# Masks of the second score pass as a minimum on VectorE, row factors stored with the rows, experts written out

## The chip, the cores and the metric

One core of a Trainium2 chip runs the program. Its engines take their own instruction streams in order and meet through semaphores: PE (TensorE, matrix products into PSUM), DVE (VectorE, elementwise work and reductions), ACT (ScalarE, activations), POOL (GpSimd) and SP (SyncE, which here only issues transfers). The metric is the device time of one execution in microseconds (us), as the median of several runs.

## The reference

32 sequences of 512 tokens with 256 features (D) pass through an embedding, one attention block and one expert block.

```python
h = (tok_table[x] + pos_table[None] + seg_table[seg]) * sqrt(D)
h = h + attention(layernorm(h))
h = h + experts(layernorm(h))
```

Attention: 16 heads of 16 features look at a causal window of 64 to 127 keys (the own block of 64 and the one before). Eight more heads look at 64 latents, which are means over 8 tokens each; a token sees the latents up to its own. Masked scores are minus infinity ahead of the softmax. Both results are gated by a sigmoid of the query, added, and multiplied by `w_out`.

Experts: each of 8 experts in turn takes the 2048 tokens with its highest score among those not yet taken, so expert e+1 is chosen after expert e.

```python
norm = layer_norm(feat, ln_g, ln_b)
scores = norm @ centroids.T
for e in range(8):
    idx = top_k(where(taken, -inf, scores[:, e]), 2048)
    h = layer_norm(feat[idx], ln_g, ln_b)
    out[idx] = feat[idx] + gelu(h @ w1[e] + b1[e]) @ w2[e] + b2[e]
```

`feat` is itself the layer norm of the attention's output added to it, so a row needs its mean and two inverse deviations.

## The kernel before, in words

The program has three stages. **Attention** runs sequence by sequence, written out as 33 passes of `sequence` on each engine (the last pass only finishes sequence 31). **Selection** picks the first expert's tokens. **Experts** runs a loop `Fori(0, E - 1)` on every engine, with the eighth expert written out behind it; while an expert is computed, DVE and PE choose the tokens of the next.

In attention the table `plan` (ten half steps, two for each of five steps s) sets the order on all engines. One step on PE is:

- `top_scores(s)`: scores with queries on the partitions, 64 queries by 128 keys for all heads (s = 0: the latents; s = 1 to 4: the four tiles of 128 tokens, t = s - 1). They serve only to find each query's largest score.
- half step 2s: tasks of `plan`, among them VAL t (`values`: probabilities times values), WO t (output product), MX (transposes the maxima);
- `key_scores(u)` for u = s - 1: the same scores with keys on the partitions, the query's maximum taken off by a row stored in `Qt`;
- half step 2s + 1: more tasks, among them RO t (the remote heads' product).

Masks are added in PSUM by PE itself: ahead of each score pass, `top_scores` and `key_scores` issue two rounds of eight `MATMUL` of a one-hot (`onehot`) with a mask table of 512 columns in bf16 (L983, L988, L1020, L1024). ACT takes the exponential of the second pass (`act_exp`, L684) into `probT` or `latT`, in two halves called pairs. VAL t multiplies them two half steps later (L1060), and waits for the exponentials of tile t and for DVE to have emptied `V_ps`.

DVE, in program order per step: `dve_tops(s)` (maxima of `top_scores`, L1162), `dve_outputs` for VAL (L1210 to L1215), `dve_latents`, `dve_indices`, `dve_embed` (a later sequence's rows), then the tasks that DVE takes from PE: RO (L1183 `r`, L1186 `mix`), WO (L1192 `score`, L1196 `h`, then the statistics L1199 to L1203), PV. PE has three PSUM banks for the tasks (`M_ps`), so the third task behind a WO waits until DVE has read it out.

Row factors: attention stores only the row (`h1`, 256 floats). Its variance goes to `ve_all`; at the end of attention POOL takes the power -0.5 of all 128x128 of them at once (`rs_all`, L614), and DVE multiplies the scores with it (L1469). In the expert stage the rows are gathered by index, and mean and variance are computed a second time: `dve_stats` (L1309 to L1316), `pool_power` (L579), `dve_scales` (L1320, L1321), after which ACT's `act_rows` (L693, L695) may start.

Of the kernel before, what the change touches and what calls it, by code (L numbers as in the profile page):

```python
# [26 lines left out]
P = 128  # L27
D = 256
# [15 lines left out]
TAKEN = -3e38  # L44
GT = 4
# [3 lines left out]
OW = HD + 1  # L49

# [7 lines left out]
def constants(S):  # L58
# [16 lines left out]
    prev_k, diag_k = np.where(r <= q, NEG, 0.0), np.where(r > q, NEG, 0.0)  # L75
    by_query = np.stack([np.concatenate([none, diag_q], 2), np.concatenate([prev_q, diag_q], 2)], 1)
    even_key = np.concatenate([diag_k, prev_k], 2)
    odd_key = np.stack([np.concatenate([none, diag_k], 2), np.concatenate([prev_k, diag_k], 2)], 1)
    step = S // NL
    half, tile, lat = np.arange(2), np.arange(tiles), np.arange(NL)  # L80
    tok = P * tile[None, None, None, :] + W * half[None, :, None, None] + rows[:, None, :, None]
    lat_query = np.where(lat > tok[..., None] // step, NEG, 0.0)
    lat_key = np.where(r > np.arange(S) // step, NEG, 0.0)
    cols = [f(ident), f(parity * HD ** -0.5), f(parity), f(parity * (NL / S)), f(unit), f(before), f(lane), f(i),
            packed(onehot), packed(by_query), packed(even_key), packed(odd_key), packed(lat_query), packed(lat_key)]
# [5 lines left out]
def tower(nc, ins, out, cin, din, widths, SEQS, S, V, F, E):  # L91
# [12 lines left out]
    with ctx:  # L104
# [8 lines left out]
        def sem(name):  # L113
            return ctx.enter_context(nc.semaphore(name))

        h1_rows = nc.dram_tensor("h1_rows", [TOK, D], F32, kind="Internal").ap()
# [11 lines left out]
        (c_ident, c_query, c_parity, c_latent, c_unit, c_before, c_lane, c_part, onehot, by_query, even_key, odd_key,  # L128
         lat_query, lat_key) = (cst[:, int(at[n]):int(at[n + 1])] for n in range(len(widths)))
        onehot = onehot.bitcast(BF16).rearrange("p (r m) -> p r m", r=2)  # L130
        by_query = by_query.bitcast(BF16).rearrange("p (v r k) -> p v r k", v=2, r=2)
        even_key = even_key.bitcast(BF16).rearrange("p (r q) -> p r q", r=2)
        odd_key = odd_key.bitcast(BF16).rearrange("p (v r q) -> p v r q", v=2, r=2)
        lat_query = lat_query.bitcast(BF16).rearrange("p (a r t n) -> p a r t n", a=2, r=2, t=TS)
        lat_key = lat_key.bitcast(BF16).rearrange("p (r q) -> p r q", r=2)
# [17 lines left out]
        h1 = sb("h1", [P, 2, D])  # L153
        st1 = sb("st1", [P, 6])
        mv1 = sb("mv1", [P, 2])
        ve_all = sb("ve_all", [P, NT])
        rs_all = sb("rs_all", [P, NT])
# [33 lines left out]
        st2 = sb("st2", [P, GT, 6])  # L191
        mv2 = sb("mv2", [P, GT, 2])
        ve2 = sb("ve2", [P, 2, GT])
        rs2 = sb("rs2", [P, 2, GT])
        r1 = sb("r1", [P, GT])
        nmr = sb("nmr", [P, 2, GT])
# [58 lines left out]
        hrow = sb("hrow", [P, 2, GT, D])  # L255
# [17 lines left out]
        s_gr = [sem(f"s_gr{q}") for q in range(GT)]  # L273
        s_var2 = sem("s_var2")
        s_rs2 = sem("s_rs2")
        s_scales = sem("s_scales")
# [34 lines left out]
        s_exp = sem("s_exp")  # L311
        s_PV = sem("s_PV")
# [5 lines left out]
        s_rs1 = sem("s_rs1")  # L318
        s_std = sem("s_std")
# [113 lines left out]
        def _(sp):  # L433
# [21 lines left out]
            def store(b, q):  # L455
                m = Misc(b, q % 2)
                for half in plan:
# [35 lines left out]
            with sp.Fori(0, E - 1) as e:  # L493
# [34 lines left out]

        def pool_gather(pool, gi, q, idx, col):
# [7 lines left out]
                bass.IndirectOffsetOnAxis(idx[:, col:col + 1], 0)).then_inc(s_gr[q], 16)  # L537

        def pool_expert(pool, e, last):
            for g in range(GR):  # L540
# [13 lines left out]
                if g + 1 < GR:  # L554
                    pool_power(pool, gi + 1)
                for q in range(GT):
# [3 lines left out]
                    if (g, q) == (GR - 1, 1) and not last:  # L560
                        pool_power(pool, gi + 1)
# [955 lines left out]
```

## Time and profile before

| | |
|---|---|
| median of 3 runs | 3060.79 us (3056.66 to 3068.5) |
| the profiled execution's own time | 3072.49 us |
| its span, first to last instruction | 3070.7 us |
| PE busy | 2708.5 us (88%) |
| DVE busy | 1803.7 us (59%) |
| ACT busy | 1270.0 us (41%) |
| POOL busy | 874.1 us (28%) |

A row of a timeline gives the start in us from the span's start, the duration, the engine, the line of the kernel, the operation, its output and inputs with their shapes, and in brackets how long the engine was idle before it and what ended that. "issue" means that the profile shows nothing the engine waited for. In a row with x2 the duration covers both instructions. Matmul ends are modelled; starts are recorded. PEclk is the share of TensorE's full clock of 2.4 GHz that was granted.

### The profile page before, as it was taken

How to read it: one execution, taken by the hardware profiler on the slowest of the kernel's cores; microseconds unless marked ns; L12 is line 12 of the kernel's file. 1: busy time of each engine (PE TensorE's matmuls, PEld its weight loads, DVE VectorE, ACT ScalarE, POOL GpSimd, SP SyncE). 2: the span in 40 equal slices, each digit the busy share in tenths (PEclk: the TensorE clock that was granted, in tenths of full speed). 3: DMA queues.
4: the chain of work that ended last, by engine and by line, in shares of the span. 5: the costliest groups of instructions: out<-in, count | busy, mean ns of one | idle time of the engine just before them, and what ended most of it. 6: DMA issues, size and time to landing. Idle time of an engine off the chain costs nothing. (4 is left out here: it accounts for less than half of the span.)

```text
span 3070.7 us, 111586 instructions
## 1 busy us (share of the span) xinstructions
PE 2708.5 (88%) x48136; PEld 1876.3 (61%) x48136; DVE 1803.7 (59%) x5986; ACT 1270.0 (41%) x2665; POOL 874.1 (28%) x938
## 2 busy tenths in 40 slices
PE   2899999999999999999999996069999999999998
PEld 1566666666666666667676665036556655655666
DVE  3556556556565565565565643766667576676721
ACT  1444444444444444444444441033434334344343
POOL 2312112113122122121131201124353444534443
PEclk9999999999999999999999997579999999999999
DMA  2000000000000000000000001001120101111020
GB/s 64 21 23 23 21 23 25 20 23 25 22 23 23 21 25 23 23 25 20 23 25 21 23 18 42 0 28 42 47 65 29 60 31 64 54 44 57 31 67 28
DMA packets 56335, 97.59 MB, mean 32 GB/s; under 512 B 10332, under 2 KB 41000, under 8 KB 55752
## 3 DMA queue, kind: packets, MB, share of 16 engines
q0 software_dynamic: 18624, 50.88, 5.8%
q1 hardware_dynamic: 37256, 40.07, 3.9%
q8 instruction: 355, 5.82, 0.8%
q14 instruction: 100, 0.82, 0.1%
HBM read 55.78 MB, written 33.55 MB: 29 GB/s over the span
## 5 line engine op out<-in xcount | busy, mean ns | idle before, releaser
L511 POOL DMA_INDIRECT rows<-in_tok_table,idx_now x132 | 138.3, 1048 | 1355.4 <-DVE hres L1140 1251.3
L900 PE MATMUL banks<-hT,w 128*128 128x512 f32 x1024 | 476.1, 611 | 18.5 <-ACT hT L710 12.1
L1162 DVE TENSOR_REDUCE mx<-banks 128x8 f32<-128x1024 f32 x256 | 301.6, 1220 | 219.0 <-PE banks L1003 219.0
L684 ACT ACTIVATE probT<-banks 128x1024 f32<-128x1024 f32 x256 | 262.5, 1026 | 229.8 <-PE banks L1047 229.8
L721 ACT ACTIVATE hid<-banks,b 128x512 f32<-128x512 f32 x256 | 175.2, 687 | 418.0 <-PE banks L900 417.9
L900 PEld LDWEIGHTS banks<-hT,w 128*128 128x128 f32 x1024 | 188.9, 193 | 224.6 <-issue 209.9
L1060 PE MATMUL V_ps<-Vo,probT 128*64 128x17 f32 x4096 | 270.2, 212 | 3.4 <-issue 3.3
L1060 PE MATMUL V_ps<-Ve,probT 128*64 128x17 f32 x4096 | 270.0, 212 | 3.2 <-issue 2.9
L1060 PEld LDWEIGHTS V_ps<-Ve,probT 128*64 128x64 f32 x4096 | 255.5, 140 | 27.5 <-issue 27.3
L1237 DVE TENSOR_SCALAR_CACHE_REDUCE hits<-act_s,cval 128x128 bf16<-128x128 f32 x960 | 261.2, 342 | 2.3
L1060 PEld LDWEIGHTS V_ps<-Vo,probT 128*64 128x64 f32 x4096 | 255.6, 140 | 3.8 <-issue 3.8
L913 PE MATMUL M_ps<-w,hid 128*128 128x256 f32 x1024 | 231.6, 379 | 0.0
L913 PE MATMUL V_ps<-w,hid 128*128 128x256 f32 x1024 | 231.5, 379 | 0.0
L913 PEld LDWEIGHTS V_ps<-w,hid 128*128 128x128 f32 x1024 | 192.7, 190 | 38.9 <-issue 15.3
L1183 DVE TENSOR_TENSOR r<-M_ps,sg 128x256 f32<-128x256 f32 x128 | 54.4, 425 | 265.0 <-PE M_ps L789 264.0
L913 PEld LDWEIGHTS M_ps<-w,hid 128*128 128x128 f32 x1024 | 190.3, 190 | 23.6
L563 POOL TENSOR_TENSOR orow<-orow,b 128x256 f32<-128x256 f32 x128 | 126.6, 989 | 228.0 <-DVE orow L1355 226.4
L1041 PE MATMUL banks<-Qt,Kt 32*64 32x128 f32 x4096 | 186.6, 283 | 0.6 <-issue 0.6
L650 ACT ACTIVATE low<-M_ps 8x256 f32<-8x256 f32 x128 | 47.7, 372 | 335.0 <-PE M_ps L783 335.0
L1043 PE MATMUL banks<-Qt,Kt 32*64 32x64 f32 x4096 | 175.8, 227 | 3.0 <-issue 3.0
L1041 PEld LDWEIGHTS banks<-Qt,Kt 32*64 32x64 f32 x4096 | 165.1, 131 | 21.8 <-issue 2.4
L567 POOL DMA_INDIRECT out_rows<-orow,idx_cur x128 | 144.6, 1129 | 109.6 <-POOL orow L563 73.4
(227 smaller groups left out, 5676.3 us busy)
## 6 DMA issues: line engine op xcount, KB each, us to landing
h_rows<-h SPq DMA_DIRECT2D x128, 128.0 KB, 2.1
w<-in_w SPq DMA_DIRECT2D x16, 1024.0 KB, 5.4
Qt<-low SPq DMA_DIRECT2D x256, 4.0 KB
rows<-in_tok_table,idx_now POOLq DMA_INDIRECT x132, 3.5
out_rows<-orow,idx_cur POOLq DMA_INDIRECT x128, 2.5
cst<-in_tables SPq DMA_DIRECT2D x1, 1060.5 KB
Gq<-lowl SPq DMA_DIRECT2D x64, 8.0 KB
b<-in_b SPq DMA_DIRECT2D x8, 128.0 KB, 4.8
```

The lines of the kernel that those rows point to most:

```text
L511: nc.gpsimd.indirect_dma_start(rows[:, t, :], None, ins["tok_table"], bass.IndirectOffsetOnAxis(idx_now[:, t:t + 1], 0)).then_inc(s_rows[t ...
L563: nc.gpsimd.tensor_tensor(out=orow[:, q % 2, :], in0=orow[:, q % 2, :], in1=b2[:, :], op=ALU.add).then_inc(s_add, 1)
L567: nc.gpsimd.indirect_dma_start(out, bass.IndirectOffsetOnAxis(idx_cur[:, g * GT + q:g * GT + q + 1], 0), orow[:, q % 2, :], None).then_inc ...
L684: nc.scalar.activation(dst[:, 2 * pair:2 * pair + 2, :], banks[:, 2 * pair:2 * pair + 2, :], ACT.Exp).then_inc(s_exp, 1)
L721: nc.scalar.activation(hid[:, m, :], S_ps[m % 2][:, 0:GT * P], ACT.Gelu_apprx_tanh, bias=b1[:, m:m + 1]).then_inc(s_hid, 1)
L900: mm = nc.tensor.matmul(S_ps[m % 2][:, 0:GT * P], w1[:, c, m * P:(m + 1) * P], hT[g % 2][:, c, :], start=c == 0, stop=c == KC - 1)
L913: mm = nc.tensor.matmul(O_ps[q % 2][:, 0:D], hid[:, m, q * P:(q + 1) * P], w2[:, m, :], start=m == 0, stop=m == FC - 1)
L1041: nc.tensor.matmul(banks[side[0], g, n * P:(n + 1) * P], k[:, W + at_:P + at_], q[:, at_:at_ + P], start=False, stop=n == G - 1)
L1043: nc.tensor.matmul(banks[side[1], g, n * P:n * P + W], k[:, at_:W + at_], q[:, at_:at_ + W], start=False, stop=False)
L1060: nc.tensor.matmul(V_ps[side[a], h * OW:(h + 1) * OW], probT[t % 2][:, g, n * P + a * W:n * P + (a + 1) * W], vals[:, t, h, :], start=True ...
L1162: nc.vector.tensor_reduce(tops.rearrange("p (g h) -> p g h", g=2), banks[:, 2 * pair:2 * pair + 2, :].rearrange("p g (h k) -> p g h k", h= ...
L1237: ins_ = nc.vector.tensor_scalar(hits[:, c, :], act_s[:, :], cval[:, c:c + 1].bitcast(F32), None, ALU.is_ge, ALU.add, accum_out=counts[:, ...
```

## The change

- **Masks of the second pass.** `key_scores` no longer issues mask products (80 `MATMUL` of 512 columns fewer per sequence). Instead DVE takes the minimum of the exponentials with a table of 0 and 3e38 in fp32 (`dve_keep`, two instructions of 128x1024 per pass, ten per sequence), and VAL waits for that (`s_keep`) instead of the exponentials.
- **One round of latent masks.** `top_scores(0)` issues one round of eight mask products instead of two.
- **Factors with the rows.** A stored row has 260 floats: the last four are the factors of the expert stage, written by POOL in `pool_factors` behind each WO (four small operations); POOL also multiplies the scores. `rs_all`, `dve_stats`, `pool_power` and `dve_scales` are gone. SP's store of the row waits for the factors (`s_fac`), ACT waits for the gathered rows alone (`s_gr`).
- **Experts written out.** `Fori` becomes a Python loop on all five engines.

The diff, cut to its core:

```diff
+    keep_key = np.stack([np.where(np.concatenate([upper & prev & first | ~upper & diag, upper & diag | ~upper & prev], 1),
+                                  KEEP, 0.0) for first in (False, True)], 1)
+    keep_lat = np.where(key <= np.arange(S)[None, :] // step, KEEP, 0.0)
...
                         if name == "WO" and m.here(task):
-                            sp.wait_ge(s_mD, m.out(task))
+                            sp.wait_ge(s_fac, TS * (b - lag(task)) + t + 1)
                             sp.dma_start(h1_tiles[:, bass.ds(TS * (b - lag(task)) + t, 1), :],
                                          h1[:, t % 2, :].unsqueeze(1)).then_inc(s_h1out[t % 2], 16)
...
+        def pool_factors(pool, n, t):
+            own = h1[:, t % 2, :]
+            pool.wait_ge(s_var1, n + t + 1)
+            nc.gpsimd.tensor_tensor(out=own[:, D:D + 2], in0=ve1[:, t % 2, :], in1=mhalf[:, :].to_broadcast([P, 2]),
+                                    op=ALU.pow).then_inc(s_rs1, 1)
+            pool.wait_ge(s_rs1, n + t + 1)
+            nc.gpsimd.tensor_scalar(own[:, D + 2:D + 4], own[:, D:D + 2], mv1[:, t % 2, 0:1], -1.0,
+                                    ALU.mult, ALU.mult).then_inc(s_nm1, 1)
+            new = score[:, :, bass.ds(n + t, 1)]
+            nc.gpsimd.tensor_tensor(out=new, in0=new, in1=own[:, D:D + 1].unsqueeze(1).to_broadcast([P, E, 1]),
+                                    op=ALU.mult).then_inc(s_score, 1)
+            pool.wait_ge(s_nm1, n + t + 1)
+            nc.gpsimd.tensor_scalar(own[:, D + 1:D + 2], own[:, D + 1:D + 2], 1.0, None, ALU.add).then_inc(s_fac, 1)
...
-            pool.wait_ge(s_var1, NT)
-            nc.gpsimd.tensor_tensor(out=rs_all[:, :], in0=ve_all[:, :], in1=mhalf[:, :].to_broadcast([P, NT]),
-                                    op=ALU.pow).then_inc(s_rs1, 1)
             pool.wait_ge(s_next, 1)
             for q in range(GT):
                 pool_gather(pool, 0, q, idx_next, q)
-            pool_power(pool, 0)
-            with pool.Fori(0, E - 1) as e:
-                pool_expert(pool, e, False)
-            pool_expert(pool, E - 1, True)
+            for e in range(E):
+                pool_expert(pool, e, e == E - 1)
...
-        def act_rows(act, gi, q, half):
-            if q == 0:
-                act.wait_ge(s_scales, gi + 1)
+        def act_rows(act, gi, pair, q, half):
+            row = hrow[:, half, q, :]
+            act.wait_ge(s_gr[half][q], 16 * pair + 16)
...
             def key_scores(b, par, u, drained):
                 pe.wait_ge(s_max, drained)
                 pe.wait_ge(s_low[u], 32 * b + 32)
                 t = u - 1
-                for r in range(2):
-                    for g in range(G):
-                        for a in range(2):
-                            if u == 0:
-                                nc.tensor.matmul(banks[side[a], g, :], onehot[strip[g], r, :], lat_key[strip[g], r, :],
-                                                 start=r == 0, stop=False)
-                            else:
...
             def values(b, par, t):
                 pe.wait_ge(s_O, TS * b + t + 1)
-                pe.wait_ge(s_exp, 2 * (NU * b + t + 2))
+                pe.wait_ge(s_keep, 2 * (NU * b + t + 2))
...
+        def dve_keep(dve, k, u):
+            for pair in range(2):
+                dve.wait_ge(s_exp, 2 * k + pair + 1)
+                if u == 0:
+                    kept = latT[:, 2 * pair:2 * pair + 2, :]
+                    mask = keep_lat.unsqueeze(1).to_broadcast([P, 2, S])
+                else:
+                    kept = probT[(u - 1) % 2][:, 2 * pair:2 * pair + 2, :].rearrange("p g (n q) -> p (g n) q", q=P)
+                    mask = keep_key[:, min(u - 1, 1), :].unsqueeze(1).to_broadcast([P, 2 * G, P])
+                nc.vector.tensor_tensor(kept, kept, mask, ALU.min).then_inc(s_keep, 1)
...
                     for task in half:
                         dve_misc(dve, m, task, b, q, base)
+                    if n % 2 and (m.old if n == 1 else m.new):
+                        dve_keep(dve, NU * b + n // 2 - 1, (n // 2 - 1) % NU)
...
-            dve.wait_ge(s_rs1, 1)
-            chain(dve, nc.vector.tensor_tensor(score[:, :, :], score[:, :, :],
-                                               rs_all[:, :].unsqueeze(1).to_broadcast([P, E, NT]), ALU.mult), base)
+            dve.wait_ge(s_score, NT)
             chain(dve, nc.vector.tensor_tensor(score[:, :, :], score[:, :, :],
                                                kb[:, :].unsqueeze(2).to_broadcast([P, E, NT]), ALU.add), base)
```

How the instructions move, at the two places that matter most.

DVE, from RO 2 in half step 1 to VAL 3 in half step 2 (`r` and `mix` are RO's two operations, `mx` the maxima of the next tile, `sg` the first operation on VAL's result). Before:

```order
L1183 TENSOR_TENSOR r<-M_ps,sg 128x256 [waits s_misc]
L1186 TENSOR_TENSOR mix<-loc,r 128x256 [waits s_mD]
L1162 TENSOR_REDUCE mx<-banks 128x8 [waits s_S] x2
L1210 TENSOR_SCALAR sg<-gt 128x32 [waits s_PV]
L1211 RECIPROCAL rc<-V_ps 128x24
```

And in the changed kernel:

```order
L1189 TENSOR_TENSOR r<-M_ps,sg 128x256 [waits s_misc]
L1192 TENSOR_TENSOR mix<-loc,r 128x256 [waits s_mD]
L1170 TENSOR_TENSOR probT<-probT,cst 128x1024 [waits s_exp] x2
L1156 TENSOR_REDUCE mx<-banks 128x8 [waits s_S] x2
L1216 TENSOR_SCALAR sg<-gt 128x32 [waits s_PV]
```

The two minima stand behind `mix` and ahead of the maxima. The same five rows follow one another at the other half steps with an RO; in half step 5, which has none, the minima follow `dve_embed`.

POOL, in half steps 8 and 9, where WO 0 falls between two norms (`rs`, `std`, `xn`) of a later sequence. Before:

```order
L511 DMA rows<-in_tok_table,idx_now 128x256
L518 TENSOR_TENSOR rs<-ve,mhalf 128x1
L524 TENSOR_TENSOR std<-ve,rs 128x1
L526 TENSOR_SCALAR xn<-hres,mv,rs 128x256
L518 TENSOR_TENSOR rs<-ve,mhalf 128x1
```

And in the changed kernel:

```order
L510 DMA rows<-in_tok_table,idx_now 128x256
L517 TENSOR_TENSOR rs<-ve,mhalf 128x1
L523 TENSOR_TENSOR std<-ve,rs 128x1
L525 TENSOR_SCALAR xn<-hres,mv,rs 128x256
L532 TENSOR_TENSOR h<-ve,mhalf 128x2
L536 TENSOR_SCALAR h<-h,mv 128x2
L539 TENSOR_TENSOR score<-score,h 128x8
L543 TENSOR_SCALAR h<-h 128x1
L517 TENSOR_TENSOR rs<-ve,mhalf 128x1
```

Four operations are added behind each WO, ahead of the last norm in this case and in a stretch without other POOL work for WO 1 to 3.

## Rows read from the trace of the kernel before

**Rows 1.** Busy time by engine in most of attention; each time with its instruction count

```profile
core 0: us, PE busy (x) PEld busy (x) DVE busy (x) ACT busy (x) POOL busy (x), PEclk, DMA share, GB/s
150.00:1870.00 1720.00, 1616.47 (x41613) 1163.39 (x41619) 1010.11 (x2530) 812.50 (x1780) 350.51 (x464) 0.99 0.08 22
```

**Rows 2.** Timeline of PE: the latents' second pass, mask products and then scores

```profile
1229.86 0.64 PE L1020 MATMUL banks<-cst 32*64 32x512 bf16 x16
1230.32 1.04 PE L1030 MATMUL banks<-Gq,Gk 32*64 32x512 f32 x16
```

**Rows 3.** Timeline of DVE in the setup: 1024 elements, two operands and one

```profile
25.36 1.23 DVE L1382 TENSOR_TENSOR P<-P,segs 128x1024 f32<-128x1024 f32 x1
27.08 0.69 DVE L1385 TENSOR_SCALAR P<-P 128x1024 f32<-128x1024 f32 x1
```

**Rows 4.** Timelines of DVE and PE, step 1: RO 2, maxima, VAL 3, Q 1

```profile
1224.74 0.42 DVE L1186 TENSOR_TENSOR mix<-loc,r 128x256 f32<-128x256 f32 x1
1225.77 2.36 DVE L1162 TENSOR_REDUCE mx<-banks 128x8 f32<-128x1024 f32 x2 [0.60 <-PE banks L1003]
...
1226.10 0.23 PE L1060 MATMUL V_ps<-Ve,probT 128*64 128x17 f32 x1
...
1232.28 1.12 PE L804 MATMUL M_ps<-x1T,wq 128*128 128x512 f32 x2 [0.67 <-DVE h L1196]
```

**Rows 5.** Timelines of DVE and PE, step 2: RO 3, MX 2

```profile
1235.19 0.42 DVE L1186 TENSOR_TENSOR mix<-loc,r 128x256 f32<-128x256 f32 x1
...
1239.69 0.39 PE L783 MATMUL M_ps<-cst,mx 128*8 128x128 f32 x2
```

**Rows 6.** Timelines, steps 3 and 4: top scores 3, VAL 0, RO 0, VAL 1, V 1

```profile
1246.29 0.65 PE L988 MATMUL banks<-cst 32*64 32x512 bf16 x16 [1.46 <-ACT probT L684]
...
1256.42 0.42 DVE L1186 TENSOR_TENSOR mix<-loc,r 128x256 f32<-128x256 f32 x1
...
1257.74 0.23 PE L1060 MATMUL V_ps<-Ve,probT 128*64 128x17 f32 x1
...
1264.28 1.01 PE L816 MATMUL M_ps<-wvg,x1T 128*128 128x296 f32 x3 [0.46 <-DVE h L1196]
```

**Rows 7.** Timelines of DVE and PE, step 0: RO 1, VAL 2

```profile
1268.96 0.42 DVE L1186 TENSOR_TENSOR mix<-loc,r 128x256 f32<-128x256 f32 x1
...
1271.13 0.23 PE L1060 MATMUL V_ps<-Ve,probT 128*64 128x17 f32 x1
```

**Rows 8.** Timelines of DVE and POOL at the end of attention

```profile
1908.53 0.15 DVE L1203 TENSOR_SCALAR ve_all<-mv 128x1 f32<-128x1 f32 x1
...
1909.54 20.75 POOL L614 TENSOR_TENSOR rs_all<-ve_all,mhalf 128x128 f32<-128x128 f32 x1 [134.31 <-DMA h_rows<-h]
...
1931.69 1.22 DVE L1471 TENSOR_TENSOR score<-score,kb 128x1024 f32<-128x1024 f32 x1
```

**Rows 9.** Groups of instructions on POOL: powers of one column, small product

```profile
L518 POOL TENSOR_TENSOR rs<-ve,mhalf 128x1 f32<-128x1 f32 x128 | 73.9, 577 | 2.9
...
L524 POOL TENSOR_TENSOR std<-ve,rs 128x1 f32<-128x1 f32 x128 | 24.1, 188 | 26.4 <-POOL rs L518 20.7 <-PE M_ps L812 4.8 <-PE M_ps L816 0.6
```

**Rows 10.** Timelines of DVE and ACT: the first expert's rows arrive, ACT starts

```profile
2014.20 0.43 DVE L1309 BATCH_NORM_STATS2 st<-hrow 128x6 f32<-128x256 f32 x1 [3.76 <-DMA hrow<-h_rows,idx_next]
...
2021.31 0.60 ACT L693 ACTIVATE y<-hrow,nmr,rs 128x256 f32<-128x256 f32 x1 [116.49 <-DVE nmr L1321]
```

**Rows 11.** Waits of PE in the expert stage: total us, times, longest us

```profile
PE banks L887 <- ACT y L693: 22.9, 20, 11.9
PE M_ps L826 <- DVE hits L1237: 22.8, 14, 2.3
PE M_ps L845 <- DVE ohB L1288: 12.6, 14, 1.4
PE banks L900 <- ACT hT L710: 12.1, 8, 1.6
PE banks L900 <- ACT hid L721: 6.4, 6, 1.4
```

**Rows 12.** Timelines of DVE and PE where the loop turns from expert to expert

```profile
2294.24 0.17 DVE L1328 COPY b<-b_all 128x8 f32 x1 [3.75 <-issue]
...
2299.62 0.18 PE L826 MATMUL M_ps<-counts,onesb 128*128 128x15 bf16 x1 [1.08 <-DVE hits L1237]
```

**Rows 13.** Timelines of POOL in step 4, and of DVE in the expert stage

```profile
1255.30 1.22 POOL L526 TENSOR_SCALAR xn<-hres,mv,rs 128x256 f32<-128x256 f32 x1
...
2061.69 1.10 DVE L1247 TENSOR_TENSOR thr<-thr,delta 128x1 int32<-128x1 int32 x1
```

More of the change, by code:

```diff
@@ L272, in tower @@
         s_cur = sem("s_cur")
[L273 to L276, printed above, removed]
+        s_gr = [[sem(f"s_gr{j}{q}") for q in range(GT)] for j in range(2)]
         s_scaled = sem("s_scaled")
@@ L492, in _ @@
             sp.dma_start(b2[:, :], ins["b2"][0:1, :].to_broadcast([P, D])).then_inc(s_b2, 16)
-            with sp.Fori(0, E - 1) as e:
+            for e in range(E - 1):
                 src1 = w1_v[:, bass.ds(e + 1, 1), :, :].rearrange("p a c f -> p (a c) f")
@@ L604, in sequence @@
                         pool_norm(pool, b + 2, NORM_AT[n], (q + 2) % HB, m)
+                    for task in half:
+                        name, t = task
+                        if name == "WO" and m.here(task):
+                            pool_factors(pool, TS * (b - lag(task)), t)
             sequence(0, 0)
@@ L723, in act_expert @@
                 if g + 1 < GR or not last:
-                    act_group(act, gi + 1, g + 1 if g + 1 < GR else 0)
+                    act_group(act, gi + 1, GR // 2 * e + (g + 1) // 2, g + 1 if g + 1 < GR else 0)
         @block.scalar
@@ L755, in _ @@
             nc.scalar.activation(scr[:, :], c_ident[:, 0:1], ACT.Copy).then_inc(s_hid, 2)
-            act_group(act, 0, 0)
-            with act.Fori(0, E - 1) as e:
-                act_expert(act, e, False)
-            act_expert(act, E - 1, True)
+            act_group(act, 0, 0, 0)
+            for e in range(E):
+                act_expert(act, e, e == E - 1)
         def pe_misc(pe, m, task, b):
@@ L992, in top_scores @@
-                for n in range(2 * TS if s == 0 else G):
-                    j, c = divmod(n, TS if s == 0 else KC)
+                            nc.tensor.matmul(banks[side[a], g, :].rearrange("p (h k) -> p h k", h=G), onehot[strip[g], r, :],
+                                             by_query[strip[g], min(t, 1) if a == 0 else 1, r, :].unsqueeze(1)
+                                             .to_broadcast([32, G, P]), start=r == 0, stop=False)
+                for n in range(G):
+                    j, c = divmod(n, KC)
@@ L1007, in top_scores @@
-                        if g % 2 and n == (2 * TS if s == 0 else G) - 1:
+                            at_ = t * P + a * W
+                            mm = nc.tensor.matmul(banks[side[a], g, n * P:(n + 1) * P],
+                                                  Qt[par][strip[g], j, c, at_:at_ + W],
+                                                  Kt[par][strip[g], j, c, at_:at_ + P], start=False, stop=n == G - 1)
+                        if g % 2 and n == G - 1:
                             mm.then_inc(s_S, 1)
@@ L1109, in _ @@
                 pe_rows(pe, 0, q)
-            with pe.Fori(0, E - 1) as e:
-                pe_expert(pe, e, False)
-            pe_expert(pe, E - 1, True)
+            for e in range(E):
+                pe_expert(pe, e, e == E - 1)
         CH = {"n": 0}
@@ L1285, in dve_choice @@
             elif part == "list":
-                if not (isinstance(n, int) and k < 2):
+                if not (isinstance(n, int) and n == 0 and k < 2):
                     dve.wait_ge(s_used, LC * n + k - 1)
```

193 lines of the change are left out of this document (72 added, 121 removed).

## The prediction

> **What bounds the kernel now.** I read the page first, then busy time by windows, then the timelines of one sequence in the middle, and last the waits. Attention takes 1720 of the span's 3070.7 us in the window that I read, with PE busy 94% of it at a granted clock of 0.99 (2.4 GHz) and DVE 59% [rows 1]. So a microsecond of PE's work is worth a microsecond only where nothing else ends last, and the reader has to look at the few places in a sequence where PE waits for DVE or ACT: ahead of Q 1 for 0.67 us [rows 4], ahead of the top scores 3 for 1.46 [rows 6], ahead of V 1 for 0.46 [rows 6]. There a shorter PE only waits longer. DVE has 41% to spare as an average, but the change puts work on it at fixed places: right between a task's `mix` and the next VAL. How close VAL follows `mix` today is the number that decides.
>
> **PE's products that go.** One pass of masks takes 1230.32 - 1229.86 = 0.46 us from its first product to the first score product [rows 2]. Five such passes, and the one latent round of two (0.23), are 5 x 0.46 + 0.23 = 2.53 us per sequence, 81 us over 32 sequences, if all were on the path.
>
> **DVE's minima that come.** Ten per sequence. The trace of before has no minimum of 128x1024. An fp32 operation of that shape with two operands took 1.23 us, with one operand 0.69 [rows 3]; these are the two bounds. I take 1.23: the mask is a second operand. Two are 2.46, and with a small hand-over to PE (an estimate) VAL can start 2.5 us after `mix` ends. The pair of maxima of as many elements, 2.36 [rows 4], says the same of two in a row. A sequence then goes as follows, each against its own row.
>
> Step 1: `mix` ends at 1224.74 + 0.42 = 1225.16, VAL 3 could start at 1227.66 and started at 1226.10 [rows 4]: **+1.56**. The 0.46 of the second pass isn't won back, since PE waits ahead of Q 1 for DVE, which is as late [rows 4].
>
> Step 2: `mix` ends at 1235.61 [rows 5]. Here the next reader is MX 2, which needs the maxima behind the minima: 1235.61 + 2.5 + 2.36 = 1240.47 against 1239.69 [rows 5], 0.78 late. The mask pass ahead of it gives 0.46: **+0.32**. The top scores 3 that follow wait for ACT's exponentials, which wait for PE's scores, so that wait moves along.
>
> Step 3: half step 5 has no RO, and the minima of tile 0 follow ACT's second half, behind `dve_embed`. They end about 1.3 us after the exponentials, while the mask products of the top scores 3, 1.46 us of waiting included, are still being issued [rows 6]: nothing.
>
> Steps 3 and 4: `mix` ends at 1256.84, VAL 1 could start at 1259.34 and started at 1257.74 [rows 6]: **+1.60**. V 1 waits for DVE's `h` again [rows 6], so the pass's 0.46 goes into that wait.
>
> Step 0: `mix` ends at 1269.38, VAL 2 could start at 1271.88 and started at 1271.13 [rows 7], 0.75 late, less 0.46: **+0.29**. The latents' 0.23 I count as nothing, in the same wait.
>
> The sum is 1.56 + 0.32 + 1.60 + 0.29 = 3.77 us per sequence, **+121 us** over 32. Were the 0.46 won also in the two places where I gave it up, 2.85 and +91; were it won nowhere, 4.69 and +150.
>
> **Selection.** Scores wait now for one power of 128 columns, 20.75 us [rows 8]. Afterwards only the last tile's factors are outstanding. Their power has two columns: one costs 0.577 [rows 9] and a further one 20.75 / 128 = 0.16, so 0.74, and two small operations of 0.19 [rows 9]. With the hand-over of 0.86 between DVE's variance and POOL [rows 8] the addition of `kb` starts at 1908.68 + 0.86 + 0.74 + 0.38 = 1910.66 and not at 1931.69 [rows 8]: **-21 us**, on the path in full, since DVE does nothing else there.
>
> **First expert.** Its rows were there at 2014.20, and ACT began at 2021.31 behind statistics, power and scales [rows 10]. Now ACT waits for the rows alone: **-7 us**.
>
> **Experts.** From the waits of PE [rows 11]: those for `y` are 22.9, of which 11.9 is the first expert's, counted above; 11.0 go, with the statistics. Where the loop turns, DVE stood 3.75 us with nothing that it waited for [rows 12], then seven waits for `hits` of 1.08 each follow [rows 12]: 7.6 go, the other seven stay, as they lie between two rounds of the search. Of `ohB`'s 12.6 I take 9, because DVE gets there about 4 us earlier, and of `hid` all 6.4, which stand at the turn as well. `hT` stays. Sum 34, **-34 us**; bounds: `y` and `hid` alone 17.4, with all of `ohB` and `hT` 50.
>
> **What costs nothing.** The store of a row waits for POOL's factors, about 2 us later; behind it in SP's queue stand loads for a later sequence, and nobody reads the rows before the gathers, some 100 us after the last store [rows 8, 10]. POOL's four operations per WO, 0.74 + 3 x 0.19 = 1.3 us, fit an engine that is busy 350.51 of 1720 us [rows 1]; if they delayed a norm of a later sequence, that has a step to spare. The rows' 16 further bytes ride on DMA that is busy 8% [rows 1]. PE's clock stays where it is, I think: it is 0.99 with a wait of 1.46 in every sequence [rows 1, 6].
>
> **Sum.** 121 - 21 - 7 - 34 = +59 us. The profiled execution took 3072.49 us, 11.7 above the median of 3060.79, so it would take 3131 and the median **3120 us**. The bounds are 91 - 21 - 7 - 50 = +13, 3074, and 150 - 21 - 7 - 17 = +105, 3166.
>
> **Rival: the minima are quick.** At 0.69 each [rows 3] a pair takes 1.08 us less. Then MX 2 and VAL 2 are in time and both passes there win their 0.46; VAL 3 and VAL 1 are 0.48 and 0.52 late. 1.00 - 0.92 = 0.08 per sequence, 3 us, and the rest's 62 remains: **3002 us**, faster. For it speaks that a one-operand form of the same size has that time. Against it: the row of 1.23 has the very form, two operands in fp32, and the pair of maxima is no quicker. It decides below 1.0 us per minimum: each us by which a pair is shorter takes off 4 per sequence, and 62 / 32 = 1.93 is reached when a pair is 0.46 shorter. Chance 0.10; another 0.06 for a smaller gain, 3030 to 3045, if the minima lie between or fewer places wait than I think.
>
> **Rival: nothing measurable.** The delays come to about half, because the later passes hand some slack on to the next step (two of my four terms are below 0.35 already). 121 halved is 60, against the 62 of the rest: **3060 us**. Chance 0.08.
>
> **Rival: minima that POOL holds up.** DVE has an operation of one column that took 1.10 us in the expert stage [rows 13], against 0.15 for one in attention [rows 8]; what held it the rows don't say. If each critical pair of minima were 0.95 us longer, four in a sequence, 32 x 3.8 = 122 us come on top: **3242 us**. Against it: `mix`, which also reads two operands, took its usual 0.42 at 1256.42, while POOL's `xn` ran from 1255.30 to 1256.52, and `xn` its usual 1.22 [rows 6, 13]. That is an overlap of 0.1 us, and the minima run six times as long in a row, so I keep 0.08. The Trainium skill ("GPSIMD Engine Reference", Specifications) says that POOL shares its SBUF interfaces with VectorE, with contention where a VectorE instruction has two SBUF inputs; this speaks against the change, which adds ten such instructions. By that rule, 3242; the little overlap that the trace of before shows bears out nothing of it.
>
> **Rival: the loop's turn isn't the loop.** Were DVE's 3.75 us not from the turn, `hits` and `ohB` stay, and 17 us less are won: 3137. It lies in the range and in the forecast's chance.
>
> **Chances.** The forecast, slower through late VALs, 3074 to 3166, has 0.68. With POOL's hold-up (0.08) slower by over 0.5% has 0.76. I take 0.5%, 15 us, as what a measurement of this kernel can tell from no change. Within it: 0.08. Faster: 0.10 + 0.06 = 0.16. The range from 3030 to 3166 leaves out the quick minima (0.10) and the hold-up (0.08).
>
> **What would show it.** In the changed kernel PE should wait for DVE's minimum (`probT`, L1170) about 1.6 us ahead of VAL 1 and of VAL 3 and 0.3 to 0.75 ahead of VAL 2 and MX 2, with nothing of the kind ahead of VAL 0; the 320 minima should have a mean of about 1.2 us; a sequence should take 3.8 us longer. The addition of `kb` should stand some 2 us behind the last variance, ACT's first `y` at the arrival of its rows, and the 3.75 us on DVE should be gone. I am wrong if the minima take under 1 us, if DVE runs them before the task's `mix`, or if PE's wait for them is as long as I say and a wait elsewhere shrinks by as much: then the period of a sequence shows it.

## The result, and the profile after

The changed kernel takes 3147.26 us (median of 4 runs, 3138.72 to 3156.45) against 3064.64 of the kernel before in the same session (4 runs): a ratio of 1.0267, 95% interval 1.022 to 1.0314. The profiled executions took 3156.45 and 3072.49 us, so 84 us of difference are to be found in the trace. The forecast was +59, slower, and 3120 us; the measured time lies inside the range, in part by luck, as told below.

First the page of the changed kernel, its line of busy times and the granted clock in 40 slices:

```profile
PE 2714.0 (86%) x45320; PEld 1911.6 (61%) x45320; DVE 2097.6 (66%) x5893; ACT 1266.6 (40%) x2659; POOL 1010.5 (32%) x1417
...
PEclk9999999988999998989998999757999999999999
```

PE issues fewer products and is still as busy as before. The window that answers to [rows 1], and a short one in it (columns as there):

```profile
150.00:1870.00 1720.00, 1505.80 (x35571) 1098.39 (x35570) 1252.17 (x2622) 752.13 (x1649) 534.84 (x895) 0.93 0.08 21
1258.80:1265.00 6.20, 6.20 (x77) 4.89 (x82) 4.23 (x11) 0.37 (x1) 0.00 (x0) 0.50 0.01 3
```

In the same 1720 us there are 35571 instructions on PE instead of 41613. Of the 6042 that are missing, 88 in each of some 28 sequences, about 2460, are the mask products that are gone (an estimate); the rest means that fewer sequences fit into the window. The granted clock is 0.93 instead of 0.99. The second row shows how: for 6.2 us in one sequence PE runs at 0.50, which is 1.2 GHz.

PE's waits in that window (waited for, total us, times, longest us):

```profile
PE V_ps L1055 <- DVE probT L1170: 111.1, 77, 1.9
PE banks L1002 <- ACT probT L690: 40.7, 28, 1.5
PE M_ps L788 <- ACT Gk L675: 17.7, 28, 0.6
PE M_ps L809 <- DVE h L1202: 12.3, 18, 0.7
PE M_ps L798 <- DVE mix L1192: 10.7, 28, 0.6
...
PE M_ps L821 <- DVE h L1202: 4.0, 4, 1.3
```

The first line is the wait of the forecast, VAL for the minima. The timeline of DVE and PE in one sequence, for steps 1 (VAL 3), 2 (MX 2), 4 (VAL 1, V 1) and 0 (VAL 2), answers to [rows 4 to 7]:

```profile
1255.29 0.43 DVE L1192 TENSOR_TENSOR mix<-loc,r 128x256 f32<-128x256 f32 x1
1255.63 2.35 DVE L1170 TENSOR_TENSOR probT<-probT,cst 128x1024 f32<-128x1024 f32 x2
...
1258.13 0.20 PE L1055 MATMUL V_ps<-Ve,probT 128*64 128x17 f32 x1 [1.42 <-DVE probT L1170]
...
1274.15 0.27 PE L788 MATMUL M_ps<-cst,mx 128*8 128x128 f32 x1 [0.63 <-ACT Gk L675]
...
1293.82 0.20 PE L1055 MATMUL V_ps<-Ve,probT 128*64 128x17 f32 x1 [1.88 <-DVE probT L1170]
...
1300.27 0.52 PE L821 MATMUL M_ps<-wvg,x1T 128*128 128x296 f32 x1 [0.92 <-DVE h L1202]
...
1307.30 0.20 PE L1055 MATMUL V_ps<-Ve,probT 128*64 128x17 f32 x1 [0.82 <-DVE probT L1170]
```

Ahead of MX 2 the profile names ACT's `Gk`, but before the change MX 2 started at 1239.69 [rows 5], while `Gk` was still running. What MX 2 needs are DVE's maxima, and these end at 1274.00 in the changed kernel, just ahead of 1274.15. The first row is from the changed kernel, the second from the kernel before:

```profile
1271.65 2.35 DVE L1156 TENSOR_REDUCE mx<-banks 128x8 f32<-128x1024 f32 x2
```

```profile
1239.52 0.70 ACT L669 ACTIVATE Gk<-M_ps,cst 128x64 f32<-128x64 f32 x2
```

The end of attention (DVE, POOL) and the start of the first expert (DVE, ACT), answering to [rows 8, 10]:

```profile
2071.57 0.22 DVE L1209 SCALAR_TENSOR_TENSOR ve<-eps,mv 128x2 f32<-128x2 f32 x1
2071.87 0.72 POOL L532 TENSOR_TENSOR h<-ve,mhalf 128x2 f32<-128x2 f32 x1 [4.18 <-DVE ve L1209]
2073.37 1.23 DVE L1452 TENSOR_TENSOR score<-score,kb 128x1024 f32<-128x1024 f32 x1 [1.57 <-POOL score L539]
...
2151.89 0.17 DVE L1300 TENSOR_TENSOR idx_next<-rank,M_ps 128x16 int32<-128x16 f32 x1
...
2156.79 0.60 ACT L699 ACTIVATE y<-hrow 128x256 f32<-128x256 f32 x1 [88.92 <-DMA hrow<-h_rows,idx_next]
```

And the same row of the list of tokens in the kernel before, which the table below needs:

```profile
2010.27 0.17 DVE L1294 TENSOR_TENSOR idx_next<-rank,M_ps 128x16 int32<-128x16 f32 x1
```

From these rows the spans of the stages, against the terms of the forecast:

| stretch | before | after | difference | forecast |
|---|---|---|---|---|
| start to the last variance | 1908.68 | 2071.79 | +163.1 | +121 |
| to the addition of kb | 23.0 | 1.6 | -21.4 | -21 |
| to the end of idx_next | 78.8 | 78.7 | -0.1 | 0 |
| to ACT's first y | 10.9 | 4.7 | -6.1 | -7 |
| to the end of the span | 1049.4 | 997.9 | -51.5 | -34 |
| sum | 3070.7 | 3154.7 | +84.0 | +59 |

So two terms came out as forecast, and two are larger than forecast, with opposite signs.

### The profile page after: what moved, and what is told of

Same layout as the page of the kernel before. It is cut to its first block and busy times, and to the rows that moved or that the text cites. A ratio compares the mean times of both kernels' runs of the same rounds, so it can differ in the third digit from the quotient of the medians.

```text
span 3154.7 us, 104415 instructions
## 1 busy us (share of the span) xinstructions
PE 2714.0 (86%) x45320; PEld 1911.6 (61%) x45320; DVE 2097.6 (66%) x5893; ACT 1266.6 (40%) x2659; POOL 1010.5 (32%) x1417
## 5 line engine op out<-in xcount | busy, mean ns | idle before, releaser
L902 PE MATMUL banks<-hT,w 128*128 128x512 f32 x1024 | 469.7, 607 | 11.2 <-ACT hT L716 10.8
L1055 PE MATMUL V_ps<-Ve,probT 128*64 128x17 f32 x4096 | 296.6, 221 | 128.1 <-DVE probT L1170 127.0
L532 POOL TENSOR_TENSOR h<-ve,mhalf 128x2 f32<-128x2 f32 x128 | 95.0, 742 | 901.4 <-DVE ve L1209 901.4
L1055 PEld LDWEIGHTS V_ps<-Ve,probT 128*64 128x64 f32 x4096 | 286.0, 154 | 154.3 <-issue 154.3
L1170 DVE TENSOR_TENSOR probT<-probT,cst 128x1024 f32<-128x1024 f32 x256 | 304.5, 1220 | 46.0 <-ACT probT L690 45.9
L510 POOL DMA_INDIRECT rows<-in_tok_table,idx_now x132 | 154.6, 1171 | 498.8 <-DVE hres L1134 410.0
L1055 PE MATMUL V_ps<-Vo,probT 128*64 128x17 f32 x4096 | 300.3, 222 | 0.0
L1055 PEld LDWEIGHTS V_ps<-Vo,probT 128*64 128x64 f32 x4096 | 286.8, 155 | 0.0
L1036 PE MATMUL banks<-Qt,Kt 32*64 32x128 f32 x4096 | 204.9, 299 | 0.3 <-issue 0.2
L1038 PE MATMUL banks<-Qt,Kt 32*64 32x64 f32 x4096 | 191.6, 240 | 0.0
```

The lines of the kernel that those rows point to most:

```text
L510: nc.gpsimd.indirect_dma_start(rows[:, t, :], None, ins["tok_table"], bass.IndirectOffsetOnAxis(idx_now[:, t:t + 1], 0)).then_inc(s_rows[t ...
L902: mm = nc.tensor.matmul(S_ps[m % 2][:, 0:GT * P], w1[:, c, m * P:(m + 1) * P], hT[g % 2][:, c, :], start=c == 0, stop=c == KC - 1)
L1036: nc.tensor.matmul(banks[side[0], g, n * P:(n + 1) * P], k[:, W + at_:P + at_], q[:, at_:at_ + P], start=True, stop=True)
L1038: nc.tensor.matmul(banks[side[1], g, n * P:n * P + W], k[:, at_:W + at_], q[:, at_:at_ + W], start=True, stop=True)
L1055: nc.tensor.matmul(V_ps[side[a], h * OW:(h + 1) * OW], probT[t % 2][:, g, n * P + a * W:n * P + (a + 1) * W], vals[:, t, h, :], start=True ...
L1170: nc.vector.tensor_tensor(kept, kept, mask, ALU.min).then_inc(s_keep, 1)
```

## The experiments

Each ratio is against the kernel before, run on the same chip in the same session; the medians of the kernel before were 3066.43 (the first four kernels), 3081.16 (the next four), 3072.45 (the next three) and 3069.45 us (the last).

### Masks back on PE

```diff
-                pe.wait_ge(s_keep, 2 * (NU * b + t + 2))
+                pe.wait_ge(s_exp, 2 * (NU * b + t + 2))
...
-                        dve_keep(dve, NU * b + n // 2 - 1, (n // 2 - 1) % NU)
```

and the 16 mask products per pass in `key_scores` as before.

> The changed kernel with the masks of the second pass back on PE and no minima; all else of the change stays. Theory A (the minima ahead of VAL cost attention, the rest of the change is worth what the other terms said): about 3003 us, that is 62 below the kernel before; a sequence takes 55.9 us again or up to 0.2 less, the granted clock in attention is 0.99, PE waits for no minimum. Rival B (POOL's factors and the later store cost attention too): the sequence stays above 56.5 us and the time above 3030. Rival C (the gains after attention are smaller than the terms): attention as before, but the end at 3025 to 3065.

Measured: 2993.9 us, ratio 0.9756 (0.9737 to 0.9775). The window's clock is 0.99 and no wait for minima is left:

```profile
150.00:1870.00 1720.00, 1612.59 (x41604) 1162.70 (x41605) 1023.28 (x2541) 814.51 (x1784) 529.43 (x952) 0.99 0.08 23
```

POOL is busy 529 us here, PE does about as many products as before, and the last variance comes at 1902.1 us, some 6.5 earlier than before. So factors, the later store and the written-out experts cost attention nothing that can be seen, and all the loss is in the minima. The gain is 72 us by the medians, a little more than the 62 of the terms.

### Minima of 8 columns

```diff
-                    kept = latT[:, 2 * pair:2 * pair + 2, :]
+                    kept = latT[:, 2 * pair:2 * pair + 2, 0:4]
```

and the same for `probT`.

> The changed kernel with each minimum cut from 1024 columns to 8, in its place and with its semaphore; it leaves the masks of the second pass out. Theory A (what costs is how long the minima stand between mix and VAL): the waits for the minima fall from 111 us to under 15, a sequence falls to between 53.4 us (all of the 2.53 us of mask products won) and 55.0 (0.92 won), the time to 2925 to 2975, the granted clock to 0.98 or more. Rival B (DVE is slowed by POOL, or the mere hand-over by one more engine costs): the waits stay above 40 us, the time above 3060. Rival D (the clock falls because PE's mask products are missing): the granted clock stays at 0.93 and the time above 3000.

Measured: 2930.62 us, ratio 0.9534 (0.9503 to 0.9565), for a kernel that leaves the masks of the second pass out; clock 0.99 up to 1700 us, no wait for minima in the list. Without mask products and with the hand-over in place nothing is lost, so neither the hand-over nor the lack of mask products explains the loss or the clock. What costs is the 2.35 us that two full minima stand ahead of VAL. It is also the mark of what free masks would be worth: 63 us below masks on PE.

### The wait filled with products

```diff
+                for _ in range((0, 3, 1, 3)[t]):
+                    nc.tensor.matmul(V_ps[:, 0:D], c_ident, wq[:, 0, :], start=True, stop=True)
                 pe.wait_ge(s_keep, 2 * (NU * b + t + 2))
```

> The changed kernel with products that nothing reads (128x128 by 128x256 in fp32, 0.42 us each) put on PE where it waits for the minima: three ahead of VAL 1 and VAL 3, one ahead of VAL 2. Theory A' (PE's stand ahead of VAL is what lets the granted clock fall to 1.2 GHz for some 6 us of most sequences): the granted clock in attention goes from 0.93 to 0.97 or more, a sequence takes about 2 us less, the time is about 3080. Rival D (the clock falls for want of the mask products, or for another reason): the clock stays at 0.93 and the time at 3147 or up to 20 above.

Measured: 3057.66 us, ratio 0.9959 (0.9943 to 0.9975). Seven useless products per sequence make the changed kernel 90 us faster. The window, and behind it the waits:

```profile
150.00:1870.00 1720.00, 1569.97 (x37938) 1143.89 (x37940) 1317.82 (x2759) 799.55 (x1738) 595.34 (x940) 1.00 0.08 22
```

```profile
PE M_ps L821 <- DVE h L1204: 24.5, 26, 1.3
PE V_ps L1057 <- DVE probT L1172: 21.4, 53, 0.5
PE M_ps L809 <- DVE h L1204: 21.1, 30, 1.0
```

The clock is 1.00. VAL still waits for the minima behind the filling (21.4 us in all), so the filling delays nothing there. This parts the 163 us of attention: here the addition of kb starts at

```profile
1976.35 1.23 DVE L1454 TENSOR_TENSOR score<-score,kb 128x1024 f32<-128x1024 f32 x1 [1.58 <-POOL score L539]
```

which is 1974.8 for the last variance, 66 us later than before. So 66 us, 2.06 per sequence, are the stands themselves, less what the missing mask products give back, and about 97, 3.0 per sequence, are the clock that falls behind the stands.

### First minimum ahead of r

```diff
+                        dve_keep(dve, NU * b + n // 2 - 1, (n // 2 - 1) % NU, (0,))
                     for task in half:
                         dve_misc(dve, m, task, b, q, base)
...
+                        dve_keep(dve, NU * b + n // 2 - 1, (n // 2 - 1) % NU, (1,))
```

> The changed kernel with the first minimum of each pass ahead of the tasks of its half step on DVE (ahead of r and mix) and only the second behind mix; same work. DVE stands idle for 2.2 to 2.7 us ahead of r at three of the four places, so Theory A (place, not amount): VAL 3 and VAL 2 start 1.2 us earlier, VAL 1 does not (there DVE has no idle time); with the clock back a sequence takes about 56 us and the time is 3005 to 3035, with the clock staying at 0.93 about 3065. Rival B (amount: DVE's ten minima cost by their sum, wherever they stand): 3140 to 3155.

Measured: 3059.95 us, ratio 0.9958 (0.9935 to 0.9981), with the clock at 0.95. The same ten minima cost 87 us less, so it is not their amount. The waits show where the rest sits:

```profile
PE M_ps L798 <- DVE mix L1192: 49.4, 29, 2.0
...
PE V_ps L1055 <- DVE probT L1170: 29.6, 59, 0.7
```

Where DVE has no idle time ahead of `r` (half step 7), the earlier minimum pushes `mix`, and PE stands ahead of MT 0, which needs it, and so less ahead of VAL 1.

### Experts written out, alone

```diff
-            with dve.Fori(0, E - 1) as e:
-                dve_expert(dve, e, False, PER2 * e + base)
+            for e in range(E - 1):
+                dve_expert(dve, e, False, base)
```

on the kernel before, and the same on the four other engines.

> The kernel before with nothing changed but the expert loop written out on the five engines. From the addition of kb to the end the changed kernel is 57.7 us shorter than the kernel before, where the terms said 41. Theory A (the terms, the loop's turn on PE's waits only: 7.6 + 9 + 6.4): 23 us less, about 3043. Rival E (the 17 us that were missing in the sum belong to the turn too, since all engines and the clock start again there): 35 to 42 us less, about 3027. Rival F (they belong to the statistics that are gone): 23 us or less here.

Measured: 3068.76 us, ratio 0.9964 (0.9942 to 0.9985), 11 us (5 to 18). PE's waits in the expert stage, to be held against [rows 11]:

```profile
PE banks L887 <- ACT y L693: 23.6, 21, 12.0
PE M_ps L826 <- DVE hits L1237: 18.7, 15, 2.5
PE M_ps L845 <- DVE ohB L1288: 12.8, 14, 1.6
PE banks L900 <- ACT hT L710: 10.8, 8, 1.4
```

`hid` is gone (6.4) and `hits` shorter by 4, but `ohB` stays. DVE's stands of 3.75 us [rows 12], 23.8 in all before, are gone from its waits. In the changed kernel, where the statistics are gone as well, the list reads:

```profile
PE M_ps L831 <- DVE hits L1243: 15.9, 19, 1.9
PE banks L902 <- ACT hT L716: 10.8, 8, 1.4
PE banks L889 <- ACT y L699: 8.1, 4, 5.8
PE banks L902 <- ACT hid L727: 0.4, 1, 0.4
```

So `ohB` does not go with the loop alone; with the statistics gone too, it does. DVE's own waits in the kernel before point to the reason, which no run shows by itself: ahead of the scales DVE stood for POOL's power, with the search for the next expert queued behind it:

```profile
DVE r L1320 <- POOL rs L579: 46.6, 32, 1.8
```

### VAL later on PE

```diff
-            [("MT", 2), ("VAL", 3), ("WO", 2), ("MX", 1)],
+            [("MT", 2), ("WO", 2), ("VAL", 3), ("MX", 1)],
```

in half steps 2 and 8, and VAL 2 behind the ET tasks in half step 0.

> The changed kernel with VAL later in PE's order alone: behind WO in half steps 2 and 8, behind the last two ET in half step 0, so that PE has 1.16 us (0.6 for VAL 2) of other work while DVE takes the minima; DVE's order is as it was. Theory A (VAL starts when the minima end, and Q 1 and V 1 wait for DVE's h, which comes behind VAL's outputs): the waits ahead of VAL fall from 111 us to under 50, those ahead of Q 1 and V 1 rise by about 1.1 us each, the sequence without clock losses stays at 57 to 58 us; 3050 to 3065 where the clock comes back to 0.97 or more, up to 3130 where it does not. Rival G (what PE fills in is simply won): 1.16 x 2 + 0.6 = 2.9 us a sequence, 93 us and the clock: under 3000.

Measured: 3150.67 us, ratio 1.0219 (1.0178 to 1.026). The wait was moved and not removed; PE's waits now begin with

```profile
PE M_ps L821 <- DVE h L1202: 51.3, 28, 2.0
PE M_ps L809 <- DVE h L1202: 47.3, 28, 2.0
```

V 1 and Q 1, as said: 47 and 35 us more than in the changed kernel (4.0 and 12.3), while VAL's own wait for the minima is down to 4.6 us. What fell short is the time: the clock came back only to 0.96, and new waits for POOL's `xn` (19.6 us) and ACT's `mixT` (31.7) appeared.

### VAL and WO exchanged on both engines

```diff
+                    early = [x for x in half if x[0] == "WO" and n in (2, 8)]
+                    for task in early:
+                        dve_misc(dve, m, task, b, q, base)
```

ahead of `dve_outputs`, together with the order of the run before.

> As the kernel with VAL later on PE, and DVE too takes WO's score, h and statistics in half steps 2 and 8 ahead of VAL's outputs instead of behind them. Theory A (both ends of the chain from the minima over VAL, the outputs and h to Q 1 and V 1 have to be opened): waits ahead of Q 1 and V 1 near 0 and ahead of VAL under 50 us, granted clock 0.97 or more, a sequence of 54.5 to 55.5 us, 2945 to 2985. Rival H (DVE, fuller by 12 us a sequence, is the bound now and hands the delay to RT, r and mix): a sequence stays above 56.5, the time above 3010.

Measured: 3158.33 us, ratio 1.0253 (1.0227 to 1.0279), clock 0.93: a miss. The waits of Q 1 and V 1 are gone and VAL waits 4.5 us in all, but PE stands elsewhere:

```profile
PE M_ps L779 <- POOL xn L525: 53.4, 24, 3.2
```

This looked like a lack of room on DVE; a later run, with the ET tasks left in place, shows that it was their move.

### Masks shared between PE and DVE

```diff
+                pe_mask = [not (u == 1 or u != 2 and g < KC) for g in range(G)]
...
+                    if n % 2 and n != 7 and (m.old if n == 1 else m.new):
+                        dve_keep(dve, NU * b + n // 2 - 1, (n // 2 - 1) % NU, (0, 1) if n == 5 else (0,))
```

> The changed kernel with the masks of the second pass shared: DVE takes minima only where it has idle time (both of tile 0, and the first of tile 2, of tile 3 and of the latents, ahead of r), PE adds its mask products for the rest (tile 1, and half of the three others), so PE issues 1.15 us less of them per sequence than the kernel before. Theory A (place decides): no waits for minima, granted clock 0.98 or more; against the kernel with all masks on PE (2994) between 0.46 and 1.15 us a sequence less: 2957 to 2980. Rival B (each minimum costs, wherever it stands): above 2994.

Measured: 2972.31 us, ratio 0.9641 (0.9617 to 0.9666), clock 0.98, no wait for minima: as Theory A said. Five minima per sequence cost nothing where DVE stands idle.

### One minimum more

The same with `u in (1, 3)`, and both minima of half step 9 ahead of `r`.

> The kernel with shared masks, and one minimum more: DVE takes both of tile 2 ahead of r (there it stands idle for 2.7 us), PE adds none of its masks. Theory A (place decides): 0.23 us a sequence less on PE, no wait for the minima, 2960 to 2972. Rival (the second minimum reaches into r and mix, and VAL 2 or the top scores of the latents wait): 2972 to 3000, with a wait for mix or the minima of 0.3 us or more per sequence.

Measured: 2957.78 us, ratio 0.9625 (0.9594 to 0.9655). Its waits show none for minima and 5.5 us in all for `mix`. It is the fastest kernel of the study that leaves nothing out, 3.75% below the kernel before, but its interval and that of the former overlap.

### One latent round, alone

```diff
-                            if s == 0:
+                            if s == 0 and r == 0:
                                 nc.tensor.matmul(banks[side[a], g, :].rearrange("p (j t n) -> p j t n", j=2, t=TS),
-                                                 onehot[strip[g], r, :],
+                                                 ownhot[strip[g], side[a]],
```

> The kernel before with one round of the latents' query masks instead of two, nothing else. The prediction's term: 0.23 us a sequence on PE, swallowed by the wait that follows: 0, ratio 1.000. Rival: won in full, 32 x 0.23 = 7 us, ratio 0.998; the waits of PE for gt ahead of RO then stay as long as before.

Measured: 3070.34 us, ratio 0.999 (0.9972 to 1.0008). The interval holds both 0 and 7 us; this stays undecided.

### VAL and WO exchanged, ET left in place

> As the kernel with VAL later on both engines, but half step 0 as in the changed kernel (VAL 2 between the ET tasks); VAL 1 and VAL 3 alone stand behind WO. In the former PE waited 53 us for POOL's xn, which the minima of half step 9 hold up (std 1.09 instead of 0.18, xn 2.21 instead of 1.22 us beside them), and the clock stayed at 0.93. Theory I (the moved ET tasks ran into the late xn, and that stand let the clock fall): xn waits under 15 us, the wait for the minima about 25 us (VAL 2 alone), clock 0.96 or more, 3000 to 3060. Rival H (DVE is the bound with the minima, wherever VAL stands): 3120 to 3160 with the clock at 0.93 to 0.95.

Measured: 3022.5 us, ratio 0.9841 (0.9805 to 0.9878), clock 0.98; the list has no line for `xn` and 20.1 us for VAL 2 on the minima. Against the changed kernel (1.0267) that is 4.1% less with the same ten minima, and against the run with the ET tasks moved (1.0253) 4.0% less by leaving these in place. Theory I holds in its signs (what made `xn` late is taken up at the end), and Rival H falls: DVE is not the bound. The kernel is that of the run with VAL and WO exchanged on both engines, without its change of half step 0.

### All on DVE, both cures

```diff
+                        dve_keep(dve, NU * b + n // 2 - 1, (n // 2 - 1) % NU, ((0,), (0,), (0, 1), (), (0, 1))[n // 2])
                     for task in half:
```

ahead of the tasks, the remaining minima behind them, with VAL and WO exchanged.

> All masks of the second pass on DVE as in the changed kernel, with both cures: VAL 1 and VAL 3 behind WO on PE and DVE, and the minima ahead of r where DVE stands idle there (both of tile 2, the first of tile 3 and of the latents; those of tile 1 stay behind mix). Theory A (place decides, the amount does not): no wait for the minima ahead of VAL 2, the clock in attention at 0.98 or more, 2940 to 2975, so level with or below the shared masks (2958). Rival (the 2 us stands of PE that the trace gives to issue, or POOL's xn behind the minima, stay): 2980 to 3020.

Measured: 2996.79 us, ratio 0.9767 (0.9751 to 0.9784), a miss: no better than masks on PE, and above the shared masks. The time lies in the rival's range. VAL waits 4.8 us in all for minima and PE 2.5 for `xn`, but the clock is 0.97, and these stay:

```profile
PE M_ps L802 <- ACT mixT L648: 35.6, 63, 0.6
PE banks L992 <- issue: 16.4, 9, 2.2
```

Waits for `mixT` of 31 to 36 us stand in all four kernels in which WO comes ahead of VAL, and in the changed kernel there are none. What PE stands for within the latents' scores stays open.

## Why the prediction was right, and where not

**The minima ahead of VAL: right in mechanism and place.** The pair takes 2.35 us where 2.46 was taken, and VAL 3, VAL 1 and VAL 2 wait 1.42, 1.88 and 0.82 us, where 1.56, 1.60 and 0.75 was said. VAL 0 waits for none, and MX 2 stands 0.63 us where 0.3 to 0.75 was said. The small minima show that the duration ahead of VAL is the cause, the split minima and the shared masks that the place counts and not the number alone.

**"PE's clock stays where it is, I think": wrong, and the largest error.** I had argued from the wait of 1.46 ahead of the top scores 3, beside which the clock stays at 0.99 [rows 1, 6]. With the waits ahead of VAL added the clock falls: after the stand of 1.42 at 1258.13 PE runs at 1.2 GHz from 1258.8 to 1265, and VAL's products take 3.95 us instead of 2.53. Each of the six sequences from 1011 to 1388 us has one to three such stretches; these two follow a VAL 1 at 1166.12, behind a stand of 1.88, and a VAL 3 at 1318.93, behind one of 1.42:

```profile
1167.00:1173.00 6.00, 6.00 (x86) 4.88 (x91) 3.68 (x10) 0.28 (x1) 0.24 (x1) 0.50 0.01 3
1320.50:1326.50 6.00, 6.00 (x57) 3.47 (x55) 4.34 (x13) 0.37 (x1) 0.00 (x0) 0.50 0.01 3
```

Filling the waits restored the clock and 90 us. This is about 97 of the 163 us, a term that the sum did not have.

**The sum of the stands, 3.77 per sequence: too large.** With the clock held up they cost 2.06, and the term that was off is VAL 2's +0.29. The stretch from V 1 to the next Q 0, in which VAL 2 lies, is 1.26 us shorter in the filled kernel than before (means of 29 sequences: 13.11 and 14.37), while the rest of the sequence is 3.11 longer, where the other three terms make 3.48 (together 1.85 for the sequences between 150 and 1870 us). One such stretch before, V 1 and Q 0:

```profile
1264.28 0.52 PE L816 MATMUL M_ps<-wvg,x1T 128*128 128x296 f32 x1 [0.46 <-DVE h L1196]
...
1278.24 0.59 PE L804 MATMUL M_ps<-x1T,wq 128*128 128x512 f32 x1
```

And in the filled kernel:

```profile
1304.14 0.52 PE L821 MATMUL M_ps<-wvg,x1T 128*128 128x296 f32 x1 [0.93 <-DVE h L1204]
...
1317.06 0.59 PE L809 MATMUL M_ps<-x1T,wq 128*128 128x512 f32 x1
```

The pass (0.46) and the latents' round (0.23), which go there, are 0.69 of it; why the rest goes is not shown. Q 1 and V 1 won nothing, as said: Q 1 follows the start of VAL 3 after 5.82 to 5.96 us in 22 of 26 sequences before and after 5.82 or 5.83 in 29 of 30 of the filled kernel. (The 6.18 of [rows 4] is one of the exceptions.) In step 2 the size was right and the place wrong: the only pass between VAL 3 and MX 2 is that of [rows 2], given up in step 1, but the pass behind MX 2 is won (MX 2 to K 0: 1239.69 to 1241.86 before, 1277.93 to 1279.68 filled).

**Selection and first expert: right** (-21.4 for -21, -6.1 for -7).

**Experts, -34: too small, -51.5, and one reason of it was wrong.** PE's waits less the first expert's fell by 35.5 us, so the sum of the waits was right, though not its parts: `ohB` lost all of its 12.6 and `y` 8.7 of 11.0. But "7.6 go" for `hits` and 9 for `ohB` "because DVE gets there about 4 us earlier" at the turn is not how: writing the loop out alone is worth 11 us, leaves `ohB` at 12.8 and `hits` at 18.7. `ohB` is gone only where the statistics are, behind whose wait for POOL the search stood. The 16 us above the waits lie in PE's busy time, which fell from 973.5 to 958.1 us for the same 4315 products, with the mean clock of the stage going from 0.98 to 0.99; a part of that may be PE running less at half clock behind shorter stands, which I had not priced here either; no run parts it.

**Luck.** That the time lies inside the range owes something to errors of opposite sign. The stands cost 66 us where 121 was said, the clock 97 where nothing was, and the experts gave 51.5 where 34 was said. Attention as a whole, +163, lies above the +150 that the upper bound allowed, and the experts' gain lies beyond the 50 of theirs.

**The rivals.** Quick minima: no, they take 1.22. Nothing measurable: no. The loop's turn isn't the loop: half right; DVE's stand was the loop's, but `ohB` and most of `hits` stay without it. POOL's hold-up of the minima: no, the hold-up is there the other way round, as the section on the hardware shows; so 3242 was a price for the wrong engine.

## What to carry to other kernels

Work that is moved to an engine with time to spare is paid by the wait that it stretches, so look for the place where the receiver stands idle ahead of the consumer and put it there: ten minima behind `mix` cost 163 us, their stands and the clock together, and five or six ahead of `r` or in idle time cost nothing that can be seen. A stand of the matrix engine has two prices, its own length and the products behind it at half clock; here the second was the larger. When a wait is moved, follow the chain behind it to its end, since VAL later on one engine only moved the wait to Q 1 and V 1.

## What the runs showed of the hardware

**The clock.** Waits of 1.42 to 1.88 us ahead of VAL, beside others in the sequence, let the granted clock fall to 1.2 GHz, mostly for 4 to 7 us; one wait of 1.46 per sequence alone does not (0.99 before). What it takes between these the runs do not say. PE also stands within the latents' scores with nothing shown that it waits for: 7.1 us in all before (L998, up to 1.4), 7.5 in the changed kernel and 16 to 21 in the three kernels with VAL and WO exchanged on both engines (up to 2.2); the cause is open.

**POOL stands for DVE's minima, and DVE's minima hardly for POOL.** Half step 9 of the changed kernel on DVE and POOL:

```profile
1304.80 2.35 DVE L1170 TENSOR_TENSOR probT<-probT,cst 128x1024 f32<-128x1024 f32 x2
...
1304.98 1.09 POOL L523 TENSOR_TENSOR std<-ve,rs 128x1 f32<-128x1 f32 x1 [0.20 <-POOL rs L517]
1306.06 2.21 POOL L525 TENSOR_SCALAR xn<-hres,mv,rs 128x256 f32<-128x256 f32 x1
```

`std` ends with the first minimum, and `xn` takes 1.0 us more than its usual 1.22 [rows 13], about what was left of the second. Over the window `std` has a mean of 305 ns instead of 188 [rows 9], while the minima keep theirs (one of the 224 took 1.41):

```profile
L1170 DVE TENSOR_TENSOR probT<-probT,cst 128x1024 f32<-128x1024 f32 x224 | 266.5, 1220 | 35.9 <-ACT probT L690 35.9
```

Where ET 2 and ET 3 had been moved ahead of VAL 2 (53.4 us), this is only a part of what made `xn` late. There it is the factors' operations, four of which stand ahead of the last `xn`, that the minima hold up; `h` has a mean of 905 ns instead of 745, and `xn` keeps 1227:

```profile
1308.73 1.33 POOL L532 TENSOR_TENSOR h<-ve,mhalf 128x2 f32<-128x2 f32 x1
...
1312.09 1.23 POOL L525 TENSOR_SCALAR xn<-hres,mv,rs 128x256 f32<-128x256 f32 x1
```

The four take 2.4 us in this place, some 0.8 of it hold-up, and no run parts that from their own length.

By the Trainium skill ("SBUF — State Buffer", SBUF: two separate sides) VectorE's second pair of ports is shared with GpSimd as an exclusive lock that the first to start holds for its whole instruction; the trace of the changed kernel agrees for the two rows of POOL, and the mean of 1220 ns shows no such delay of the minima.
